# Pre-norm attention and gated feed-forward block: q and k with tokens on the partitions, and the small f32 products as four column tiles

## The reference

```python
def _layernorm(x, scale, bias):               # over the HD = 8 features of a head
    mean = jnp.mean(x32, axis=-1, keepdims=True)
    var = jnp.mean(jnp.square(x32 - mean), axis=-1, keepdims=True)
    return (x32 - mean) * jax.lax.rsqrt(var + EPS) * scale + bias
q = (x @ Wq + bq).reshape(b, s, NH, HD)       # k and v alike
q, k, v = _layernorm(q, q_scale, q_bias), _layernorm(k, ...), _layernorm(v, ...)
probs = jax.nn.softmax(jnp.einsum('bqhd,bkhd->bhqk', q, k) * scale, axis=-1)
out = jnp.einsum('bhqk,bkhd->bqhd', probs, v).reshape(b, s, NH * HD) @ Wo + bo
...
h = jax.nn.silu(einsum('bsd,hd->bsh', x, wg)) * einsum('bsd,hd->bsh', x, wu)
return einsum('bsh,dh->bsd', h, wd)           # 384 hidden features, int weights / 127
...
x = x + attention(layernorm(x)); x = x + ffn(layernorm(x))
```

## Time and profile before

| | us |
|---|---|
| median of three executions | 410.79 (409.46 to 411.71) |
| profiled execution, its own time | 411.5 |
| its span, first to last instruction | 409.7 |
| PE busy (matmuls) | 373.8 (91%) |
| ACT busy | 280.9 (69%) |
| DVE busy | 242.8 (59%) |
| POOL busy | 49.1 (12%) |
| granted TensorE clock, mean over the span | 0.954 |

### The profile page before, as it was taken

How to read it: one execution, slowest core, us unless ns; L and a number is a source line. 1 busy time by engine, 2 the same in 40 slices (tenths; PEclk the granted TensorE clock), 3 DMA queues, 4 the chain that set the end, 5 groups by cost and what they waited for, 6 DMA issues and landing times.

```text
span 409.7 us, 7113 instructions
## 1 busy us (share of the span) xinstructions
PE 373.8 (91%) x2383; PEld 151.5 (37%) x2383; DVE 242.8 (59%) x617; ACT 280.9 (69%) x322; POOL 49.1 (12%) x65
## 2 busy tenths in 40 slices
PE   5865699899999999999999999999999899989866
PEld 5543323133334332533344333433253223322455
DVE  4796863479456966396648945695628552343244
ACT  1211488978777688678777877768868977888401
POOL 6400200121003100121003100310002110010010
PEclk9955699999999999999999999999999999999959
DMA  4208744044605360264406450536025522400000
GB/s 109 61 5 221 119 168 86 21 85 154 104 2 105 134 137 15 61 144 116 64 0 128 154 102 0 102 107 141 7 65 118 137 42 63 69 1 2 27 0 26
DMA packets 32948, 32.81 MB, mean 80 GB/s; under 512 B 3608, under 2 KB 29848, under 8 KB 32920
## 3 DMA queue, kind: packets, MB, share of 16 engines
q1 hardware_dynamic: 32056, 32.19, 34.1%
q10 hardware_dynamic: 864, 0.26, 0.3%
HBM read 17.76 MB, written 14.68 MB: 79 GB/s over the span
## 4 chain that ended last, share of the span: by engine, by line
PE 71%; DVE 13%; ACT 6%; issue 4%; DMA 3%; POOL 1%; SPq 1%; POOLq 0%; DVEq 0%; ACTq 0%
PE oacc L719 25%; PE scores L705 13%; PE side L686 10%; ACT probs L576 6%; PE side L693 5%; DVE xn L879 5%; PE side L632 4%; PE side L645 4%; PE side L650 3%; PE side L658 2%; PE side L677 2%; DMA kst<-parts_dram 1%; DVE qk_n L961 1%; PE scores L797 1%; DMA x_in<-in_L_attn_x 1%
## 5 line engine op out<-in xcount | busy, mean ns | idle before, releaser
L576 ACT ACTIVATE probs<-scores 128x1024 f32<-128x1024 f32 x256 | 248.1, 1023 | 75.2 <-PE scores L705 73.9
L719 PE MATMUL oacc<-probs,vaug 128*32 128x512 f32 x1024 | 136.2, 604 | 1.3 <-ACT osb L549 1.2
L705 PE MATMUL scores<-qst,kst 50*128 50x512 bf16 x512 | 82.2, 386 | 10.5 <-DMA kst<-parts_dram 4.9
L705 PEld LDWEIGHTS scores<-qst,kst 50*128 50x128 bf16 x512 | 16.6, 94 | 123.4 <-ACT probs L576 114.7
L475 POOL TENSOR_SCALAR ve<-mv 128x4 f32<-128x4 f32 (+1 forms) x17 | 5.4, 316 | 285.8 <-DVE mv L873 285.7
L719 PEld LDWEIGHTS oacc<-probs,vaug 128*32 128x32 f32 x1024 | 20.4, 108 | 46.7 <-ACT probs L576 33.6
L1041 DVE SCALAR_TENSOR_TENSOR ga<-th,side 128x512 f32<-128x512 f32 x21 | 14.3, 683 | 26.6 <-ACT th L544 26.6
L1058 DVE TENSOR_TENSOR y<-side,x 128x512 f32<-128x512 f32 x7 | 4.8, 692 | 36.1 <-PE side L693 36.1
L1048 DVE TENSOR_TENSOR hT<-side,ga 128x512 f32<-128x512 f32 x23 | 15.8, 691 | 16.6 <-PE side L686 16.6
L686 PE MATMUL side<-x2T,wgT 128*128 128x512 f32 x42 | 23.6, 644 | 0.0
L686 PE MATMUL side<-x2T,wuT 128*128 128x512 f32 x42 | 23.6, 644 | 0.0
(11 more groups left out here) (128 smaller groups left out, 390.8 us busy)
## 6 DMA issues: line engine op xcount, KB each, us to landing
parts_dram<-parts SPq DMA_DIRECT2D x24, 256.0 KB, 2.5
qst<-parts_dram SPq DMA_DIRECT2D x32, 192.0 KB, 4.7
kst<-parts_dram SPq DMA_DIRECT2D x32, 192.0 KB, 5.3
parts_dram<-parts SPq DMA_DIRECT2D x8, 384.0 KB, 2.6
parts_dram<-parts SPq DMA_DIRECT2D x24, 128.0 KB, 1.9
x_in<-in_L_attn_x SPq DMA_DIRECT2D x8, 256.0 KB, 2.6
x_res<-in_L_attn_x SPq DMA_DIRECT2D x8, 256.0 KB, 5.4
out_dram<-y SPq DMA_DIRECT2D x8, 256.0 KB, 2.1
```

Source lines behind the costliest of these rows:

```text
L576: act.activation(probs[:, kt, 2 * c:2 * c + 2, :], scores[:, 2 * c:2 * c + 2, :], ACT.Exp)\
L705: last = pe.matmul(scores[:, 2 * c + parity, :], kst[r, pair, kt * P:(kt + 1) * P], qst[r, pair, :], start=True, stop=True)
L719: last = pe.matmul(oacc[STRIP * j:STRIP * (j + 1), :], vaug[:, kt, NG * g + j, :], probs[:, kt, j, :], start=first, stop=last_of_half)
```

## The change

The q and k products are made like v's: 128 tokens on the partitions, four token tiles side by side. The head sums of their squares come from DVE (`sums_qk`, new) and the pieces `e_var0` and `e_var1` are gone, with their constants and waits. DVE multiplies q and k with 1/sqrt in that layout (`heads_normed`, new), PE transposes the product in `a_rq` and `a_rk`, and DVE applies scale and bias straight from PSUM (`affined`). Biases of q and k are broadcast rows, loaded and centred together with the weights.

Every product of a side piece (v, q, k, Wo, gate, up, down) goes through a new helper `strips`: four matmuls with 32 weight columns each, each on its own strip. In u = 10 the transposes `c_OT0` now stand ahead of `b_g1`; bank numbers change; `silu_up(i-1, 0)` moves behind `variances`. The products of the tail, the transposes, `scores_of`, `times_v`, the DMAs of q and k and ACT's order stay.

```diff
 SIDE = {0: ["a_v"], 1: ["a_rq"], 2: ["b_OT1", "a_rk"], 3: ["b_onT", "e_xT"], 4: ["b_Wo"], 5: ["e_q"], 6: ["e_k"],
-        7: ["b_x2T", "e_var0"], 8: ["b_g0"], 9: ["b_u0", "e_var1"], 10: ["b_g1", "c_OT0"], 11: ["b_u1"],
+        7: ["b_x2T"], 8: ["b_g0"], 9: ["b_u0"], 10: ["c_OT0", "b_g1"], 11: ["b_u1"],
         12: ["b_g2"], 13: ["b_u2"], 14: ["b_d0"], 15: ["b_d1"]}
...
-        wraw = sb("wraw", [P, 4, D])
+        wraw = sb("wraw", [P, 6, D])
...
+            def strips(out, weights, moving, start=True, stop=True):
+
+                for c in range(NG):
+                    cols = slice(STRIP * c, STRIP * (c + 1))
+                    last = pe.matmul(out[cols, :], weights[:, cols], moving, start=start, stop=stop)
+                return last
...
-                elif what in ("q", "k"):
-                    pe.wait_ge(xnT_done, b + 1)
-                    w = 0 if what == "q" else 1
-                    pe.matmul(bank, wqkv[:, w, :], xnT[:, :], start=True, stop=True)\
-                      .then_inc(q_filled if what == "q" else k_filled, 1)
-                elif what == "v":
+                elif what in ("q", "k", "v"):
                     pe.wait_ge(xnT_done, b + 1)
                     for t in range(NT):
-                        last = pe.matmul(bank[:, t * D:(t + 1) * D], xnT[:, t * P:(t + 1) * P], wqkv[:, 2, :],
-                                         start=True, stop=True)
-                    last.then_inc(v_filled, 1)
-                elif what in ("var0", "var1"):
...
+                        last = strips(bank[:, t * D:(t + 1) * D], xnT[:, t * P:(t + 1) * P],
+                                      wqkv[:, "qkv".index(what), :])
+                    last.then_inc({"q": q_filled, "k": k_filled, "v": v_filled}[what], 1)
...
-                    pe.matmul(bank, (wgT if what[0] == "g" else wuT)[:, j, :], x2T[:, :], start=True, stop=True)\
+                    strips(bank, (wgT if what[0] == "g" else wuT)[:, j, :], x2T[:, :])\
...
+            def sums_qk(b):
+                dve.wait_ge(qksq_done, 2 * (b + 1))
+                dve.reduce_sum(qk_sum[:, :], qk_sq[:, :, :, :].rearrange("p w t (h d) -> p (w t h) d", d=HD), AX.X)\
+                   .then_inc(qksum_done, 1)
...
+            def heads_normed(b):
+                dve.wait_ge(rsqrt_done, b + 1)
+                for w in range(2):
+                    dve.tensor_tensor(out=qk_n[:, w, :, :].rearrange("p t (h d) -> p (t h) d", d=HD),
...
-            def normed(b, w):
+            def affined(b, w):
                 name = ("a_rq", "a_rk")[w]
                 dve.wait_ge(r_filled, 2 * b + w + 1)
-                dve.tensor_tensor(out=qk_n[:, w, :], in0=side[:, BANK[name], :], in1=qk_c[:, w, :], op=ALU.mult)\
-                   .then_inc(qkn_done, 1)
                 sc, bi = ((q_aff[:, 0:1], q_aff[:, 1:2]), (affine[:, 2:3], affine[:, 3:4]))[w]
-                dve.wait_ge(qkn_done, 2 * b + w + 1)
-                dve.tensor_scalar(qk_f[:, w, :], qk_n[:, w, :], sc, bi, ALU.mult, ALU.add).then_inc(qkf_done, 1)
+                dve.tensor_scalar(qk_f[:, w, :], side[:, BANK[name], :], sc, bi, ALU.mult, ALU.add).then_inc(qkf_done, 1)
```

More of the change, by code:

```diff
@@ L603, in _ @@
         def _(pe):
-            pe.wait_ge(filled, 4)
+            pe.wait_ge(filled, 3)
             for _ in range(WARM_UP):
                 pe.matmul(scores[:, 3, 0:P], ident[:, :], ident[:, :], start=True, stop=True)
[L607 to L611, removed]
             def prepare_later_weights():
-                pe.wait_ge(bias_centred, 1)
                 for m, w in enumerate((wg_f, wu_f, wd_f)):
@@ L641, in piece @@
                     transposes(bank, lambda t: xn[:, t, :]).then_inc(xT_filled, 1)
[L642 to L647 removed]
+                elif what in ("q", "k", "v"):
                     pe.wait_ge(xnT_done, b + 1)
                     for t in range(NT):
[L650 to L661 removed]
+                        last = strips(bank[:, t * D:(t + 1) * D], xnT[:, t * P:(t + 1) * P],
+                                      wqkv[:, "qkv".index(what), :])
+                    last.then_inc({"q": q_filled, "k": k_filled, "v": v_filled}[what], 1)
                 elif what in ("rq", "rk"):
                     w = 0 if what == "rq" else 1
[L665 to L667 removed]
+                    pe.wait_ge(qkn_done, 2 * b + w + 1)
+                    transposes(bank, lambda t: qk_n[:, w, t, :]).then_inc(r_filled, 1)
                 elif what[:2] == "OT":
@@ L676, in piece @@
                     for t in range(NT):
-                        last = pe.matmul(bank[:, t * D:(t + 1) * D], onT[:, t * P:(t + 1) * P], wo[:, :],
-                                         start=True, stop=True)
+                        last = strips(bank[:, t * D:(t + 1) * D], onT[:, t * P:(t + 1) * P], wo[:, :])
                     last.then_inc(Wo_filled, 1)
@@ L692, in piece @@
                         for j in range(NF):
-                            last = pe.matmul(bank[:, t * D:(t + 1) * D], hT[:, j, t * P:(t + 1) * P], wdT[:, j, :],
-                                             start=(j == 0), stop=(j == NF - 1))
+                            last = strips(bank[:, t * D:(t + 1) * D], hT[:, j, t * P:(t + 1) * P], wdT[:, j, :],
+                                          start=(j == 0), stop=(j == NF - 1))
                     if half == 1:
```

123 lines of the change are left out of this document (50 added, 73 removed).

## The result

The changed kernel takes 392.57 us (median of 4 executions, 392.08 to 393.06), the kernel before 411.25 beside it (409.46 to 411.81). The ratio is 0.955, with a 95% interval of 0.952 to 0.959. The forecast was 389.5 with a range of 384 to 409, so the time is 3.1 us above the forecast and inside the range. The profiled execution took 392.9 us.

The account below looks back on a forecast made before the run. PE was taken to bound full turns (43.71 of 44.46 us busy), ACT turn 0. Savings 18.0 + 0.7 + 1.7 + 1.5 - 0.5 = 21.4 took the profiled 411.5 to 390.1, giving a 389.5 us median; range 384 to 409.

Parts of the forecast that it names:

- A full turn, 3.6 less: Full loop turn of 44.46 us: savings of strips, variance pieces and waits together 3.7, taken as 3.6 us.
- Unit 9: Loses its variance piece, but `times_v` waits for ACT's `copy_o`: 3.1 us, so 0.3 less instead of 1.0.
- Unit 3: PE's wait for `divide` shrinks as DVE does one multiplication less ahead of it: 0.5 us less per full turn.
- Unit 8: Gate product in strips followed by `times_v`: 2.40 us against 2.59, so 0.19 less.
- The margin of 0.4 us for the last `hT`: DVE's reordered work: the last `hT` must be ready for unit 14, with 0.4 us to spare.
- Five full turns, 18.0: Turns 1 to 5, all taken as full turns saving 3.6 us each: 18.0 us less.
- Turn 0, 0.7 less: Turn 0, otherwise bound by ACT: strips for v, q and k save 0.7 us.
- The first 44 us, +0.5: Start of the kernel: added centring, reduction and last Newton step outweigh two removed multiplications, net 0.5 us longer.
- small strips don't run side by side: Rival: 128-column load-matmul pairs pass one after another, 0.51 us per group, about 540 us in all; chance 0.13.
- the loads that don't hide: Rival: strip loads stay exposed at 128 columns, 0.03 us more per group, 10 to 11 us, 400; chance 0.10.
- PE's program no longer stays loaded: Rival: four loop jumps back wait for code, 2.5 us and more each, 10 us lost, 400; chance 0.04.
- PE waits for others: Rival: DVE's order or ACT's copy holds PE 0.7 us in units 8, 9, 14 over five turns, 400; chance 0.14.

Follow-up runs that it names:

- the kernel with the filler: Changed kernel plus four unused 128 x 128 identity products on PE in units 7 and 9 of turn 0 alone: 390.92 us, ratio 0.952.

## Why the prediction was right, and where it was off

- **A full turn, 3.6 less: 3.55.** The group of four strips with 128 columns measured 0.111 us where I took 0.107 from bounds of 0.107 and 0.51. The v, Wo, q and k units came to 2.41 (2.40 forecast), down to 2.84 (2.82), gate and up to 2.39 (2.40). That layout and strips give their gains apart was shown by a run of each. How a strip product's gain divides into load and standing rests on two rows: with a whole-tile piece behind them the strips of unit 9 took 1.00, with `times_v` behind them 0.88, so 0.12 is the standing; no run took the load away by itself.
- **Unit 7: 2.12**, as forecast. **Unit 9**: 3.1 forecast, 3.00 measured with `times_v` waiting for the copy, which ends 188.52 + 0.59 = 189.11, 1.95 us into the unit, the same 1.94 as before. **Unit 3**: 0.46 less for 0.5; the wait for `divide` is gone.
- **Unit 8** missed its 0.19: it fell by 0.02 only. The strips start at 185.31, 0.71 behind the scores, when DVE's x2T copy is through (184.48 + 0.68 = 185.16 below). I had 0.1 per turn for such waits; it was 0.17.
- **DVE**: 29.5 forecast, 29.93 measured. The reduction took 1.22 for 1.2; scale and bias read from PSUM cost 0.80 each where I had left them at their old price. The margin of 0.4 us for the last `hT` was exact: it ends at 199.76 + 0.69 = 200.45, and the down product starts at 200.85.

DVE and ACT in turn 3 of the changed kernel, in order of time:

```profile
184.48 0.68 DVE L996 COPY x2T<-side 128x512 f32<-128x512 f32 x1
185.40 1.22 DVE L876 TENSOR_REDUCE qk_sum<-qk_sq 128x128 f32<-128x1024 f32 x1 [0.23 <-ACT qk_sq L532]
...
199.76 0.69 DVE L1009 TENSOR_TENSOR hT<-side,ga 128x512 f32<-128x512 f32 x1
```

```profile
188.52 0.59 ACT L528 ACTIVATE osb<-oacc 128x512 f32<-128x512 f32 x1
```

and the group of scale and bias on DVE (busy us, mean ns of one):

```profile
L926 DVE TENSOR_SCALAR qk_f<-side,affine 128x512 f32<-128x512 f32 x8 | 6.4, 803 | 0.4 <-PE side L604 0.4
```

- **Five full turns, 18.0: 16.1.** The step that failed is "Five turns: 18.0", which took turns 1 and 2 as equal to the others. The entry of the loop cost 1.3 us of turn 1, unit 8 of turn 2 took 2.82 instead of 2.57, and the remaining 0.3 is some 0.07 per turn.
- **Turn 0, 0.7 less: 0.57 more.** The 0.7 was for v, q and k; the absence of the variance pieces in turn 0 had no term, and I had not asked what it does to the clock. Unit 10 lost 1.5 us there at the granted clock of 0.50, and was back at 2.12 in the kernel with the filler. That the idle PE is the cause stays open, as said above.
- **Turn 6, 1.7: 1.64. Turn 7, 1.5: 1.2. The first 44 us, +0.5: -0.2**; this last can't be judged, since in the ten experiments turn 0 began anywhere from 43.4 to 45.9 us.
- **The sum.** The profiled execution was forecast at 390.1 and took 392.9. The five turns, turn 0 and turn 7 together fell short by 3.5 us, and the first 44 us made good 0.7 of it, which is luck.

Of the rivals, *small strips don't run side by side* fell clearly: 0.111 us a group, with the point of decision at 0.164. So did the loads that don't hide. The Trainium skill, TensorE: Matmul & The Clock Gate (Back-to-back issue gap), has 81 ns for a pair of load and matmul with 128 columns; in strips a pair passes in 28 ns here, and with 64 columns in 14. *PE's program no longer stays loaded* was right that a longer program of PE brings a wait, and wrong on where and how often: once at the entry, 1.3 us, not at each of four jumps back. The Trainium skill, Runtime: NRT & Kernel Launch (Instruction fetch mechanics), has a taken branch stall whose target is outside a window of two pages; the jumps back showed no stall here at any length, while the entry had a gap from 460 matmuls per turn on. *PE waits for others* held only for the 0.17 in unit 8.

## What to carry to other kernels

Where an f32 product is followed by column-tiled products, issue it as column tiles as well: the load hides and the stop between shapes goes, but only if nothing with whole tiles stands between. Where something did, the strips made the unit longer (3.39 to 3.52, and 3.03 to 3.11). Price a unit from start to start of neighbouring rows; that held to 0.02 us in twelve of sixteen units. Work removed from PE at a place where another engine holds it gains less than it cost (0.4 of 1.0 in unit 9), and a stretch of idle PE can be followed by a lower granted clock, so ask of each removed piece what it was covering.

## What the runs showed of the hardware that I had not expected

- Four column tiles with 64 moving columns keep 7 ns per PE instruction over 128 instructions; no lower limit was reached.
- In turn 0 the granted clock fell to 0.50 after PE had been busy 2.33 of 4 us, in four profiles and not in two others with as long an idle PE; one that had 0.68 of 2 us kept its clock. What decides between them is open.
- Every profile entered turn 0 at a granted clock of 0.50 and kept it for 3.3 to 6.4 us with PE busy. Unit 1 took 2.34 us where that was shortest and 3.78 where it was longest.
- The first entry of a long loop cost PE 0.4 to 1.7 us, once, and varied between kernels of the same length; the jumps back cost nothing.
- DVE's scale and bias on 128 x 512 took 0.80 us from PSUM and 0.55 to 0.57 from SBUF, while a multiplication of two tensors took 0.68 with one of them in PSUM and 0.69 with none.
